# A two-layer spline network: one-sided masks, seven rounded weight tiles of sixteen, and weight differences formed on GpSimd

## Chip, cores and metric

One core of one Trainium2 chip. The time is that of the whole program on the device in microseconds; the figure compared is the median of several runs.

## The reference, cut

```python
h = concat([tokens(x), text(x_txt)])               # 32 x 164 rows of 192
h = h + attention(layernorm(h))
h = h + spline(spline(layernorm(h), w1), w2)       # 192 -> 512 -> 192
# spline(x, w): basis = cubic B-spline of x, 16 control points
#   einsum('ndk,odk->no', basis, w);  w1: (512, 192, 16), w2: (192, 512, 16)
```

The basis has finite width: of the 16 control points four are not zero for a given x. The kernel handles them as four residues r of the control point's index, each with a number n that says which of four places i the value belongs to. So the sum over 16 points is a sum over r and i of mask(n = i) times value(r) times weight(i, r).

## The kernel before

The program runs a stem with a deformed convolution, then attention, then `spline_phase`. Only the last is touched.

**First layer.** 16 pairs of batch items (`PAIRS`), each 328 rows (`PT`). A pair's work on TensorE is eight halves (`HALVES`, j), each with 36 rounded products of 328 columns (L1889 to L1891). VectorE forms the masks of a half (L1666) into a ring of four buffers `f`; `f_used` counts halves that TensorE has read. Each pair VectorE also normalises the pair after next (`norm_in`, `norm_out`), with one `power` and one `double` on GpSimd in between: its program is a loop of these two and nothing else. SP's queue loads rows (`reload`) and stores the hidden values (`leave`, four stores of 164 KB, each behind a wait for ScalarE's `empty`).

**Second layer.** 41 tiles q of 128 rows (`OT`). A tile on TensorE is four steps i; a step is 16 blocks r of 128 inputs (`4 * CH`). The first four blocks (`r < CH`, `SPLIT` = 512 columns) are split: value and weight each as a rounded high half and a low rest. The high value times high and low weight is one rounded product of 384 columns (L1911), the low value times high weight one of 192 (L1913). The other 12 blocks are plain f32 products of 192 columns (L1917), each of which the records show as two. The masked values are the stationary operand, the weights are the moving one.

VectorE's program, `tile2`, makes for each i three masks (`take2`, L1677: high, low, rest) and between them the next tile's values, 2048 columns each: `outer` (L799), `inner` (L803), `value` (L808); at the end `low2` (L1654) and the two additions of `leave` (L1736, L1739) of the tile before. Masks go into rings of four, one buffer for each i; `take2` waits until TensorE has read step i of the tile before. ScalarE works ahead: `after2` (round, `square_inner`) of tile q+2 once the masks of tile q are formed, then `before2` (four positions, three folds, `square_outer`) of tile q+3, then `high2`, which rounds the new value to its high half. Each engine takes its instructions in the order of the program text.

**The passage between the layers.** `w2` (four slices i of 1536 KB) lies where the first layer's high weights were, so slice i is loaded when TensorE has read halves 2i + 2 of the last pair. ScalarE rounds the first four blocks of each slice (`weight2_high`, L1809) and VectorE subtracts (`weight2_low`, L1703). On ScalarE the order is `high2(0,0)`, `before2(0,1,1)`, `weight2_high` 0 and 1, `after2(1,1)`, `weight2_high` 2, `before2(1,2,0)`, `empty`, `weight2_high` 3, `high2(1,1)`. On VectorE tile 0 forms the masks of i = 0, 1, 2, with `outer`, `inner` and `value` of tile 1 between, then weight 0, the mask of i = 3, and weights 1 to 3. The masks' buffers have the first layer's shape of ring, so tile 0's masks can be written from half 5 of the last pair on.

## Time and profile before

| | |
|---|---|
| median of 3 runs | 2402.74 us (2398.84 to 2403.97) |
| profiled execution, time | 2403.18 us |
| profiled execution, span | 2401.5 us |
| mean granted TensorE clock | 0.979 |
| TensorE busy | 2297.5 us, 96% |
| VectorE busy | 1878.7 us, 78% |
| ScalarE busy | 1396.5 us, 58% |
| GpSimd busy | 246.3 us, 10% |

The span runs from the first to the last recorded instruction; the time has 1.7 us more. The second layer is the stretch from 1568.9 us to the end. A matmul's end is modelled in the records and overlaps its successor, so what a product costs is read from start to start.

### The profile page before, as it was taken

The numbers are of one execution on the slowest core, as the hardware profiler recorded it, in microseconds if no ns is written. First come the engines' busy times: TensorE is split into PE (matmuls) and PEld (weight loads), VectorE is DVE, ScalarE is ACT, GpSimd is POOL, SyncE is SP. The second block draws the span as 40 slices with busy tenths as digits, with TensorE's granted clock in tenths as the row PEclk, the third lists the DMA queues.
The fourth block names the chain that finished last, engine by engine and source line by source line (L and its number), as shares of the span: only waits on it lengthen the run. The fifth ranks groups of instructions, "written<-read, shape, count | busy, mean of one in ns | idle before, by whom it ended". The sixth has DMA issues, their size and how long they took to land.

```text
span 2401.5 us, 48862 instructions
## 1 busy us (share of the span) xinstructions
PE 2297.5 (96%) x20033; PEld 2149.7 (90%) x20033; DVE 1878.7 (78%) x2364; ACT 1396.5 (58%) x1391; POOL 246.3 (10%) x133
## 2 busy tenths in 40 slices
PE   6699989999999989999999999989999999999999
PEld 5366777888888789999999999989999999999999
DVE  7699756666666587766767667589999999999995
ACT  5488303444444555435345354678888888888881
POOL 7522100000000021211212111000000000000000
PEclk9799998999999899999999999999999999999999
DMA  6655241111111100000000000210000000000000
GB/s 211 169 153 149 68 154 28 51 47 47 47 47 48 36 20 27 20 21 21 20 27 19 16 27 24 91 59 26 24 22 23 22 22 22 23 23 23 23 19 10
DMA packets 99326, 115.82 MB, mean 48 GB/s; under 512 B 15271, under 2 KB 90551, under 8 KB 98487
## 3 DMA queue, kind: packets, MB, share of 16 engines
q1 hardware_dynamic: 79087, 89.38, 12.4%
q10 hardware_dynamic: 16520, 14.34, 2.0%
q0 software_dynamic: 3616, 10.54, 1.7%
q8 instruction: 87, 1.43, 0.3%
q14 instruction: 16, 0.13, 0.0%
HBM read 83.36 MB, written 30.86 MB: 48 GB/s over the span
## 4 chain that ended last, share of the span: by engine, by line
PE 64%; issue 0%; DVE 0%
PE spline_acc L1917 27%; PE spline_acc L1890 10%; PE spline_acc L1889 10%; PE spline_acc L1891 10%; PE spline_acc L1911 5%; PE spline_acc L1913 2%; PE spline_xT L764 0%; DVE spline_f L1666 0%; DVE spline_weights_low L1649 0%; DVE spline_x L1736 0%; DVE spline_x L1739 0%
## 5 line engine op out<-in xcount | busy, mean ns | idle before, releaser
L1917 PE MATMUL spline_acc<-spline_weights,spline_f 128*128 128x192 f32 x3936 | 672.2, 328 | 0.0
L1917 PEld LDWEIGHTS spline_acc<-spline_weights,spline_f 128*128 128x128 f32 x3936 | 637.4, 190 | 0.0
L1889 PE MATMUL spline_acc<-spline_f,spline_weights_high 128*128 128x328 f32 x1536 | 480.5, 313 | 2.5 <-DVE spline_weights_low L1649 2.5
L1890 PE MATMUL spline_acc<-spline_f,spline_weights_high 128*128 128x328 f32 x1536 | 481.3, 313 | 0.0
L1891 PE MATMUL spline_acc<-spline_f,spline_weights_low 128*128 128x328 f32 x1536 | 477.7, 311 | 0.0
L1889 PEld LDWEIGHTS spline_acc<-spline_f,spline_weights_high 128*128 128x128 f32 x1536 | 289.2, 188 | 2.8 <-DVE spline_weights_low L1649 2.8
L1890 PEld LDWEIGHTS spline_acc<-spline_f,spline_weights_high 128*128 128x128 f32 x1536 | 289.4, 188 | 0.0
L1891 PEld LDWEIGHTS spline_acc<-spline_f,spline_weights_low 128*128 128x128 f32 x1536 | 289.3, 188 | 0.0
L1911 PE MATMUL spline_acc<-spline_weights_split,spline_f_high 128*128 128x384 f32 x656 | 218.2, 389 | 8.2 <-issue 8.2
L1666 DVE SCALAR_TENSOR_TENSOR spline_f<-spline_front 128x984 fp32r<-128x984 f32 x128 | 145.6, 1178 | 100.2 <-PE spline_acc L1891 94.9
L1021 DVE TENSOR_REDUCE attend_max<-scores_by_query 82x6 f32<-82x876 f32 x128 | 135.5, 1059 | 45.2 <-PE scores_by_query L1352 43.0
L1819 ACT ACTIVATE spline_hid<-spline_acc 128x328 f32<-128x328 f32 x64 | 28.1, 445 | 243.7 <-PE spline_acc L1891 243.7
L1913 PE MATMUL spline_acc<-spline_weights_split,spline_f_low 128*128 128x192 f32 x656 | 164.6, 251 | 0.0
L1194 ACT ACTIVATE attend_probs<-scores_by_key 82x1752 f32<-82x1752 f32 x64 | 104.3, 1630 | 90.1 <-PE scores_by_key L1374 90.0
L1666 DVE SCALAR_TENSOR_TENSOR spline_f<-spline_n,spline_a 128x984 fp32r<-128x984 f32 x64 | 75.6, 1181 | 99.9 <-PE spline_acc L1891 99.0
L1677 DVE SCALAR_TENSOR_TENSOR spline_f<-spline_front 128x1536 f32<-128x1536 f32 x84 | 147.1, 1752 | 0.0
L1677 DVE SCALAR_TENSOR_TENSOR spline_f<-spline_n,spline_b 128x1536 f32<-128x1536 f32 x80 | 140.1, 1751 | 0.0
L1911 PEld LDWEIGHTS spline_acc<-spline_weights_split,spline_f_high 128*128 128x128 f32 x656 | 124.0, 189 | 8.5 <-issue 8.5
L1913 PEld LDWEIGHTS spline_acc<-spline_weights_split,spline_f_low 128*128 128x128 f32 x656 | 125.7, 192 | 0.0
L574 ACT ACTIVATE spline_front<-spline_front,pixel_neg 120x576 f32<-120x576 f32 x160 | 109.7, 763 | 22.4 <-DMA spline_front<-pos_scr 22.4
L1784 ACT ACTIVATE spline_s<-spline_xn,spline_offset 128x512 f32<-128x512 f32 x160 | 101.9, 708 | 7.9 <-DMA spline_xn<-hid_scr 6.4
L551 DVE TENSOR_TENSOR hat_weights<-spline_front,spline_weights_raw 120x2880 f32<-120x2880 f32 x32 | 101.1, 3159 | 2.9 <-PE sample_acc L604 0.6
(229 smaller groups left out, 4247.6 us busy)
## 6 DMA issues: line engine op xcount, KB each, us to landing
spline_front<-pos_scr SPq DMA_DIRECT2D x32, 540.0 KB, 4.4
hid_scr<-spline_hid SPq DMA_DIRECT2D x64, 164.0 KB, 1.8
spline_xn<-hid_scr SPq DMA_DIRECT2D x41, 256.0 KB, 3.1
attend_spread<-rec_scr SPq DMA_DIRECT2D x128, 61.5 KB, 2.2
pix_scr<-spline_front SPq DMA_DIRECT2D x32, 225.0 KB
spline_weights_raw<-w SPq DMA_DIRECT2D x1, 6144.0 KB, 21.3
spline_weights<-w SPq DMA_DIRECT2D x4, 1536.0 KB, 6.2
spline_x<-h_scr SPq DMA_DIRECT2D x41, 96.0 KB, 1.9
```

The costliest lines, as they stand in the source:

```text
L574: nc.scalar.activation(dy[u][0:PIXC, part, :].rearrange("p (k n) -> p k n", k=TAPS), p[:, 0], ACT.Abs, bias=neg[0:PIXC, part:part + 1])
L1021: nc.vector.tensor_reduce(mx[0:ROWS, n, 2 * h:2 * h + 2, 0:HG], sc[0:ROWS, :, 0:SW].rearrange("p j (g n) -> p j g n", n=SPAN), AX_X, ALU.m ...
L1194: nc.scalar.activation(prT[0:ROWS, c, :, FROM[c]:FROM[c] + SPAN].rearrange("p (j g) n -> p j g n", j=4), tp[0:ROWS, :, 0:SW].rearrange("p ...
L1666: nc.vector.scalar_tensor_tensor(f[j % RING][:, part * HC:(part + 1) * HC], n_[u][:, cols], MAGIC + i, v[:, cols], ALU.is_equal, ALU.mult) ...
L1677: nc.vector.scalar_tensor_tensor(dst[:], n, MAGIC + i, v, ALU.is_equal, ALU.mult).then_inc(f_ready, 1)
L1784: nc.scalar.activation(dst[:, r * HID:(r + 1) * HID].rearrange("p (c n) -> p c n", c=CH), x2[u], ACT.Identity, bias=bias2[:, r:r + 1], sca ...
L1889: nc.tensor.matmul(z, high, x_high, start=start, stop=False)
L1890: nc.tensor.matmul(z, high, x_low, start=False, stop=False)
L1891: last = nc.tensor.matmul(z, low, x_high, start=False, stop=stop)
L1911: nc.tensor.matmul(acc2[:, u, 0:2 * D], f_high[i][:, cols], w2_split[:, i, r].rearrange("p s o -> p (s o)"), start=start, stop=False)
L1913: last = nc.tensor.matmul(z, f_low[i][:, cols], w2_split[:, i, r, 0, :], start=False, stop=False)
L1917: last = nc.tensor.matmul(z, f_rest[i][:, cols], w2[:, i, r, :], start=False, stop=stop)
```

## The change

- Masks of the second layer are one-sided: n >= i instead of n = i. The weights of slice i become the difference w2[i] - w2[i-1], so that the sum is the same. The masks for i = 0 are always one, so TensorE takes `v_high`, `v_low` and `b` themselves as operands. Values have the other sign (`minus_value`), and `leave` multiplies by -1/6.
- Seven blocks of 16 (`SETS`) are split instead of four; nine stay f32. `SPLIT` is 896 columns, the rest 1152.
- The differences for i = 1 to 3 are formed in the first layer: 36 times, SP loads two pieces of 128 x 256 from `w2`, GpSimd subtracts, SP stores the result in `step_scr`.
- The second layer's memory is laid out anew. Mask buffers exist for i = 1 to 3 only and are written once the whole first layer has been read. The raw weights of the seven blocks and the nine plain ones are loaded by separate DMAs; `weight2_high` i waits for halves 6, 7, 8, 8 of the last pair; the low halves are written over the raw ones, and lie 21.5 KB behind the high ones of the same block.
- `after2` waits, from tile 2 on, until TensorE has done step 0 of the tile two before, since it overwrites `b`.
- The orders of ScalarE and VectorE in tile 0 change.

```diff
+    SETS = 7
+    SPLIT = SETS * P
+    L1F, L1U, L2F = 2 * HALVES, HALVES, 9
+    PART = 256
+    HIGH_AT = HALVES * HALF * HID - 4 * SETS * D
...
+        HIGH_FREE = [HALVES * (PAIRS - 1) - (-(HIGH_AT + (i + 1) * SETS * D) // (HALF * HID)) for i in range(4)]
+        RAW_FREE = [HALVES * (PAIRS - 1) - (-(i + 1) * SETS * D // (HALF * HID)) for i in range(4)]
...
+            def load_step(k):
+
+                sp.dma_start(step_to[:], w2_flat[:, bass.ds(k * PART + 16 * D, PART)]).then_inc(step_in, 16)
+                sp.dma_start(step_from[:], w2_flat[:, bass.ds(k * PART, PART)]).then_inc(step_in, 16)
+
+            def leave_step(k):
+
+                sp.wait_ge(step_ready, k + 1)
+                sp.dma_start(step_flat[:, bass.ds(k * PART, PART)], step_to[:]).then_inc(step_out, 16)
+                sp.wait_ge(step_out, 16 * k + 16)
+
             reload(2)
-            with sp.Fori(0, PAIRS - 3) as t:
+            load_step(0)
+            reload(3)
+            leave(0)
+            with sp.Fori(1, PAIRS - 4) as t:
                 reload(t + 3)
-                leave(t)
+                for n in range(3):
+                    leave_step(3 * t - 3 + n)
+                    load_step(3 * t - 2 + n)
+                    if n == 1:
+                        leave(t)
...
             for i in range(4):
-                sp.wait_ge(f_used, HALVES * (PAIRS - 1) + 2 * i + 2)
-                sp.dma_start(w2[:, i], a["w2"][:, i]).then_inc(w2_in[i], 16)
+                sp.wait_ge(f_used, RAW_FREE[i])
+                sp.dma_start(w2_raw[:, i], w2_from[i][:, 0:SETS].rearrange("p r o -> p (r o)")).then_inc(w2_raw_in[i], 16)
+            for i in range(4):
+                sp.wait_ge(f_used, REST_FREE[i])
+                sp.dma_start(w2[:, i], w2_from[i][:, SETS:4 * CH]).then_inc(w2_in[i], 16)
...
-            with pool.Fori(2, PAIRS) as t:
+            def step(k):
+
+                pool.wait_ge(step_in, 32 * k + 32)
+                pool.tensor_tensor(step_to[:], step_to[:], step_from[:], ALU.subtract).then_inc(step_ready, 1)
...
+            with pool.Fori(4, PAIRS) as t:
+                for n in range(3):
+                    step(3 * (t - 4) + n)
                 front.power(pool, t)
                 front.double(pool, t)
...
-                if i == 0:
-                    dve.wait_ge(low_ready, PAIRS + q + 1)
-                dve.wait_ge(f_used, L1U * PAIRS + 4 * q + i - RING + 1)
+                dve.wait_ge(f_used, L1U * PAIRS + (4 * q + i - 3 if not (isinstance(q, int) and q == 0) else 0))
...
-                    nc.vector.scalar_tensor_tensor(dst[:], n, MAGIC + i, v, ALU.is_equal, ALU.mult).then_inc(f_ready, 1)
+                    if i == 1 and dst is f_low[1]:
+                        dve.wait_ge(low_ready, PAIRS + q + 1)
+                    nc.vector.scalar_tensor_tensor(dst[:], n, MAGIC + i, v, ALU.is_ge, ALU.mult).then_inc(f_ready, 1)
+
+            def minus_value(q, u):
+
+                dve.wait_ge(front.outer_ready, PAIRS + q + 1)
+                dve.wait_ge(front.inner_ready, PAIRS + q + 1)
+                nc.vector.scalar_tensor_tensor(b_[u][:], a_[u][:], 0.0, b_[u][:], ALU.min,
+                                               ALU.subtract).then_inc(v_ready, 1)
...
-                take2(q, u, 0)
+                if first:
+                    weight2_low(0)
+                    weight2_low(1)
+                take2(q, u, 1)
                 if more:
                     front.outer(nc, dve, PAIRS + q + 1, a_[v][:], t_[v][:])
-                take2(q, u, 1)
+                if first:
+                    weight2_low(2)
+                take2(q, u, 2)
                 if more:
                     front.inner(nc, dve, PAIRS + q + 1, b_[v][:], t_[v][:])
-                take2(q, u, 2)
-                if more:
-                    front.value(nc, dve, PAIRS + q + 1, a_[v][:], b_[v][:])
+                    minus_value(q + 1, v)
                 if first:
-                    dve.wait_ge(f_used, W2_LOW_FREE)
-                    weight2_low(0)
+                    weight2_low(3)
                 take2(q, u, 3)
-                if first:
-                    for i in range(1, 4):
-                        weight2_low(i)
...
+                if not (isinstance(q, int) and q < 2):
+                    act.wait_ge(f_used, L1U * PAIRS + 4 * q - 7)
                 front.square_inner(nc, act, PAIRS + q, b_[u][:], t_[u][:])
...
             high2(0, 0)
+            weight2_high(0)
+            weight2_high(1)
             act.wait_ge(f_ready, L1F * PAIRS)
             before2(0, 1, 1)
-            weight2_high(0)
-            weight2_high(1)
             after2(1, 1)
             weight2_high(2)
...
-                    pe.wait_ge(f_ready, L1F * PAIRS + 12 * q + 3 * i + 3)
-                    if i == 0 and not first:
-                        pe.wait_ge(y_ready, q - 1)
+                    if i == 0:
+                        pe.wait_ge(low_ready, PAIRS + q + 1)
+                        if not first:
+                            pe.wait_ge(y_ready, q - 1)
+                        high, low, rest = v_high[u], v_low[u], b_[u][:, SPLIT:C2_]
+                    else:
+                        pe.wait_ge(f_ready, L1F * PAIRS + L2F * q + 3 * i)
+                        high, low, rest = f_high[i], f_low[i], f_rest[i]
                     for r in range(4 * CH):
...
+                            both = w2_split[:, :, i, r * D:(r + 1) * D]
+                            nc.tensor.matmul(acc2[:, u, 0:2 * D], high[:, cols], both, start=start, stop=False)
+                            last = nc.tensor.matmul(z, low[:, cols], both[:, 0], start=False, stop=False)
```

## Rows read from the trace of the kernel before

**Rows 1.** The page's busy time (us, share of the span, instructions) by engine.
```profile
PE 2297.5 (96%) x20033; PEld 2149.7 (90%) x20033; DVE 1878.7 (78%) x2364; ACT 1396.5 (58%) x1391; POOL 246.3 (10%) x133
```

**Rows 2.** TensorE's waits, 800 to 2401: line, what for, us, times, longest.
```profile
PE spline_acc L1911 <- issue: 8.2, 1, 8.2
```

**Rows 3.** TensorE's timeline, second layer: start us, length us, line, operation.
```profile
1799.85 4.09 PE L1917 MATMUL spline_acc<-spline_weights,spline_f 128*128 128x192 f32 x24
1803.64 0.47 PE L1911 MATMUL spline_acc<-spline_weights_split,spline_f_high 128*128 128x384 f32 x1
...
1804.04 0.36 PE L1911 MATMUL spline_acc<-spline_weights_split,spline_f_high 128*128 128x384 f32 x1
...
1804.89 4.09 PE L1917 MATMUL spline_acc<-spline_weights,spline_f 128*128 128x192 f32 x24
```

**Rows 4.** TensorE's timeline, where the first layer ends and the second begins.
```profile
1560.31 0.31 PE L1891 MATMUL spline_acc<-spline_f,spline_weights_low 128*128 128x328 f32 x1
1568.85 0.66 PE L1911 MATMUL spline_acc<-spline_weights_split,spline_f_high 128*128 128x384 f32 x1 [8.23 <-issue]
...
1576.84 0.47 PE L1911 MATMUL spline_acc<-spline_weights_split,spline_f_high 128*128 128x384 f32 x1
```

**Rows 5.** Windows of that passage: us, busy us by engine, PEclk, DMA.
```profile
1568.80:1571.00 2.20, 2.15 (x8) 2.18 (x9) 2.20 (x3) 2.17 (x4) 0.00 (x0) 0.50 0.03 7
```

**Rows 6.** VectorE's timeline, second layer, parts of one tile.
```profile
1805.22 1.75 DVE L1677 SCALAR_TENSOR_TENSOR spline_f<-spline_front 128x1536 f32<-128x1536 f32 x1
1806.89 2.29 DVE L803 SCALAR_TENSOR_TENSOR spline_b<-spline_t,spline_b 128x2048 f32<-128x2048 f32 x1
1809.09 0.68 DVE L1677 SCALAR_TENSOR_TENSOR spline_f_high<-spline_front,spline_v_high 128x512 fp32r<-128x512 f32 x1
...
1817.04 0.69 DVE L1654 TENSOR_TENSOR spline_v_low<-spline_b,spline_v_high 128x512 fp32r<-128x512 f32 x1
1817.64 0.35 DVE L1736 SCALAR_TENSOR_TENSOR spline_x<-spline_acc,spline_x 128x192 f32<-128x192 f32 x1
...
1819.10 0.69 DVE L1677 SCALAR_TENSOR_TENSOR spline_f_high<-spline_n,spline_v_high 128x512 fp32r<-128x512 f32 x1 [0.71 <-PE spline_acc L1917]
```

**Rows 7.** ScalarE's timeline, last tile of layer one and tile 0.
```profile
1542.82 2.56 ACT L1784 ACTIVATE spline_s<-spline_xn,spline_offset 128x512 f32<-128x512 f32 x4 [1.49 <-DVE spline_f L1666]
...
1553.36 1.57 ACT L1809 ACTIVATE spline_weights_split<-spline_weights 128x768 fp32r<-128x768 f32 x2
1554.83 1.90 ACT L775 ACTIVATE spline_n<-spline_s 128x2048 f32<-128x2048 f32 x1
...
1560.38 0.82 ACT L1809 ACTIVATE spline_weights_split<-spline_weights 128x768 fp32r<-128x768 f32 x1
1567.62 2.56 ACT L1784 ACTIVATE spline_s<-spline_xn,spline_offset 128x512 f32<-128x512 f32 x4 [6.41 <-DMA spline_xn<-hid_scr]
...
1578.13 1.42 ACT L1819 ACTIVATE spline_hid<-spline_acc 128x328 f32<-128x328 f32 x4
```

**Rows 8.** VectorE's timeline, layer one: two masks, each after a half.
```profile
1522.95 1.19 DVE L1666 SCALAR_TENSOR_TENSOR spline_f<-spline_n,spline_a 128x984 fp32r<-128x984 f32 x1 [3.11 <-PE spline_acc L1891]
...
1528.34 1.18 DVE L1666 SCALAR_TENSOR_TENSOR spline_f<-spline_n,spline_a 128x984 fp32r<-128x984 f32 x1 [3.11 <-PE spline_acc L1891]
```

**Rows 9.** GpSimd and VectorE side by side, layer one.
```profile
1008.53 2.20 DVE L799 SCALAR_TENSOR_TENSOR spline_front<-spline_front 128x1968 f32<-128x1968 f32 x1
...
1008.78 6.51 POOL L745 COPY spline_xn<-spline_xn 82x256 f32<-82x256 f32 x1 [4.63 <-DVE spline_xn L686]
1046.86 1.00 POOL L739 TENSOR_TENSOR spline_rstd<-spline_ve,spline_half 82x4 f32<-82x4 f32 x1 [31.57 <-DVE spline_ve L674]
```

**Rows 10.** The page's DMA issues: KB each, median us to landing.
```profile
hid_scr<-spline_hid SPq DMA_DIRECT2D x64, 164.0 KB, 1.8
...
spline_weights<-w SPq DMA_DIRECT2D x4, 1536.0 KB, 6.2
spline_x<-h_scr SPq DMA_DIRECT2D x41, 96.0 KB, 1.9
```

94 lines of the change are left out of this document (54 added, 40 removed).

## The prediction

> **What bounds the kernel now.** I read the page first: TensorE is busy 96% of the span, VectorE 78% [rows 1]. The list of TensorE's waits then has one large entry after 860 us, 8.2 us ahead of L1911, the first matmul of the second layer [rows 2]. So both spline layers are bound by TensorE, apart from the passage between them. The timeline of the second layer gives its unit, the step: one of a tile's four values of i, 16 products. Twelve are f32, two records each: 24 records from 1799.85 to 1803.64 us, 3.79 us, 0.316 us a product. Four are rounded pairs (L1911 with L1913): 1803.64 to 1804.89 us, 1.25 us, of which the first pair has 0.40 and the other three 0.85, 0.283 each [rows 3]. A step is 5.04 us, a tile 20.16.
>
> The passage [rows 4]: layer one's last matmul starts at 1560.31 us, layer two's first at 1568.85, and the next step at 1576.84. The first step takes 7.99 us, 2.95 more than 5.04: the granted clock there is 0.50, the 1.2 GHz level, after 8.2 us without work [rows 5]. From 1576.84 on there are 163 steps of 5.04 us, which end at 2398.4; the span is 2401.5. So nothing waits in them, and tile 1 starts at 1576.84 + 3 x 5.04 = 1591.96.
>
> VectorE is nearly full in layer two [rows 6], start to start: low2 (512 columns) 0.60 us, a mask over 512 columns the same by the length of its record (0.68 against 0.69), over 1536 columns 1.67, an operation over 2048 columns 2.20, leave 0.75. Four steps of 2.87, three operations of 2.20 and the rest make 19.4 of 20.16; the 0.71 idle is the wait for TensorE. ScalarE has before2 10.54 us, after2 5.55 [rows 7] and high2.
>
> **The change, part by part.**
>
> *More rounded pairs (TensorE).* Three of twelve f32 products become pairs: 0.316 - 0.283 = 0.033 us each, 0.098 a step, so a step is 4.94 us and a tile 19.77. This is on the path for every step that doesn't wait; over the 160 steps of tiles 1 to 40 it is -15.6 us. The high half's moving operand changes its form: 384 columns in one piece before, now two runs of 192, 21.5 KB apart. No row shows that form. I price it at nothing, since the columns are as many; the first pair's excess of 0.12 us over the others [rows 3] is the nearest sign of what a change of stream can cost, so the bounds are 0 and 0.12 a pair. A gain is excluded, as it reads the same columns. I take 0.
>
> *Masks (VectorE).* From 512 and 1536 columns a column costs (1.67 - 0.60)/1024 = 1.04 ns. 896 columns then take 1.00 us, 1152 take 1.27, and one step's masks 3.28. i = 0 needs none any more (TensorE reads v_high, v_low and b), so three steps make 9.84 instead of 11.5. outer, inner and minus_value are 6.6, low2 1.0, leave 0.75; minus_value now stands right behind inner, on whose end it waits: 2.29 - 2.20, 0.1 more. The sum is 18.3 us against TensorE's 19.8: slack 1.5 where it was 0.7. No cost on the path. Uncovered, an excess over 19.8 would count whole, 40 times.
>
> *Waits.* take2(q, 1) waits until TensorE is two steps into tile q-1 and heads VectorE's queue there. Counted from the start of tile q-1 on TensorE: take2(q,1) 9.9 to 13.2, outer, take2(q,2), inner, minus_value until 23.2, take2(q,3) to 26.5, low2(q+1) to 27.5. TensorE wants them at 24.7, 29.7, 34.6 and 39.5, so 8 to 12 us spare. In after2, square_inner waits for TensorE to have read b of tile q-2, which is 4.9 us into that tile; after2 begins later, at 6.7, behind that tile's last masks. Behind it in ScalarE's queue stand before2 and high2; ScalarE's sum is 10.54 + 5.55 + about 0.95 = 17.0 of 19.8. Nothing.
>
> *GpSimd and SP in layer one.* Per pair 3 differences over 256 columns, 6 loads and 3 stores of 128 KB. GpSimd's queue has power and double behind them; SP's has reload ahead and leave(t) after the third load, with leave_step(3t-1) behind. A load or a store of such a size takes 1.9 or 1.8 us [rows 10]; a half takes 5.39 us [rows 8], a pair 43.1. The difference isn't in the trace. Nearest: double's copy of 256 columns, 6.51 us [rows 9], as long as it is because VectorE's operations run beside it; double that for two inputs, 13.0, is the upper end, and about 1 us (that copy without its delay) the lower. At 6.5 us a chain of store, load and difference is 10.2 us, three are 31 of 43: hidden, and power is wanted only some 38 us after double begins, 1008.78 to 1046.86 [rows 9]. VectorE beside the copy takes 2.20 us for 1968 columns [rows 9], no more than elsewhere, and waits 3.11 us in most halves [rows 8]. Price nothing, a gain excluded as TensorE bounds. The Trainium skill (GPSIMD Engine Reference, Key points) says that GpSimd shares its SBUF interfaces with VectorE and contends with its instructions of two SBUF inputs. By that rule the masks would be held up by the 36 differences; the trace shows the copy stretched and the mask beside it not, so by the row the charge is nothing, and by the rule it would still fall into VectorE's 3.11 us.
>
> *The passage.* Weights: the raw weights of the seven tiles are asked for after halves 1 to 4 of the last pair, the other nine's after halves 5 to 8; 884 KB land within the 6.2 us of 1536 KB [rows 10], so they are there. Halves end at 1549.8, 1555.2 and 1560.6 (steps of 5.39 back from the last). A ScalarE copy of 1344 columns is interpolated between 0.82 us at 768 and 1.90 at 2048 [rows 7]: 1.3 us, bounds 0.8 and 1.9; the subtraction on VectorE 1.5.
> - ScalarE: weight2_high(0) at 1549.8, (1) at 1555.2 to 1556.5. Only then before2(0,1,1), which ran at 1542.82 before: 1556.5 + 10.54 = 1567.1; after2(1,1) to 1572.6; weight2_high(2) to 1573.9; before2(1,2,0) to 1584.4; empty 1.4 to 1585.8; weight2_high(3) to 1587.1. The wait on the half thus moves this whole queue 13.7 us back.
> - VectorE: take2(0,0,1) must wait for layer one's end, 1560.6 to 1563.9. weight2_low(2), for ScalarE until 1573.95, to 1575.5; take2(0,0,2) to 1578.9. inner and minus_value to 1583.4; weight2_low(3) 1587.1 to 1588.6; take2(0,0,3) to 1592.0.
> - TensorE: i = 0 needs only the values and weights 0, ready by 1552.6, so it starts at 1560.5 with no wait: the 8.2 us and its 2.95 are gone. i = 0 and 1 end at 1570.4. Late next is i = 2: 1578.9, 8.5 us idle, and again a step at the low clock, 7.9 us, to 1586.8. Then i = 3 at 1592.0, 5.2 us idle. If the clock falls here too the step ends at 1599.9, else at 1597.0. I take the first, as the one wait of this length in the second layer's rows had it.
> - Tile 1 then starts at 1599.9, not 1591.96: +7.9 us. Its masks are ready at 1596.2, 1601.7 and 1609.5, against a need of 1604.8, 1609.8 and 1614.7, so no further wait.
>
> **Sum.** Profiled span 2401.5 - 15.6 + 7.9 = 2393.8, plus the 1.7 us around it = 2395.5, against 2403.18 profiled. That lies 0.44 over the median of the three runs, so 2395 for a median.
>
> **The rivals.**
> 1. *The clock doesn't fall in the second gap of tile 0.* For: it is 5.2 us against 8.2. Against: the step ahead of it has only just been at work. Tile 1 starts at 1597.0: 2392.
> 2. *The passage costs more or less than by interpolation*: the copies at their bounds move ScalarE's queue by 0.5 us each, and a longer idle before i = 2 makes nothing up. Up to +4 us: 2399. For: every term is a chain over three engines. Against: all its long terms have rows.
> 3. *A pair with a moving operand in two runs costs more.* This is the rival on the other side. One pair in each step's seven, 1120 in tiles 1 to 40, so 10 ns a pair are 11 us. The gain is gone at 7 ns and the kernel is slower by 0.2% from 11 ns on; at 20 ns the time is 2417. For: the first pair's 0.12 us. Against: that goes with the change from f32, and happens once a step now as before.
> 4. *GpSimd is late in layer one*, by the rule of contention above: from 43.1/3 - 3.7 = 10.7 us a difference, three chains are longer than a pair. At 13.0 it would be 50 of 43, 12 times, +84 us: 2479. For: the copy's 6.51 us. Against: VectorE idles in nearly every half and lets it through. The Trainium skill (GPSIMD Engine Reference, Elementwise — side-by-side cycle accounting) has 4.5 us for a sum of 2048 columns, an estimate of 0.6 for 256.
>
> **How the numbers follow.** Forecast 0.50, rival 1 0.16, rival 2 0.17, rival 3 0.13, rival 4 0.04. The predicted time is the likeliest case's, 2395. A measurement of this kernel can tell about 0.2%, 4.8 us, so faster means below 2397.9, slower above 2407.5. Rival 1 is faster, the forecast in nine of ten (it is 2.4 us from the line), rival 2 mostly same, rival 3 partly same and mostly slower. That gives faster 0.63, same 0.23, slower 0.14. The range: below, rival 1 with copies at their lower bound and the runs' spread of 2.5, 2389; above, rival 2 and the nearest part of rival 3, 2403.
>
> **What would show it.** Right: starts of steps 4.94 us apart, pairs 0.28 (rival 3: more); VectorE waiting some 1.5 us a tile, at the first mask of a tile; TensorE going on at once after layer one, then waiting about 8 us before i = 2 and 5 before i = 3 of tile 0, for VectorE's masks, with VectorE waiting there for ScalarE's weight copies; the clock at 0.50 behind both (rival 1: behind the first alone); pairs of layer one 43.1 us apart as before (rival 4: more). Wrong: a wait of TensorE in a later tile, or VectorE over 19.8 us a tile.

## The result

| | kernel before | changed kernel |
|---|---|---|
| median of 20 runs | 2397.55 us (2387.64 to 2403.97) | 2385.51 us (2376.12 to 2396.35) |
| profiled execution, time | 2403.18 us | 2391.56 us |
| profiled execution, span | 2401.5 us | 2389.8 us |

The ratio of changed to before is 0.9952, with a 95% interval of 0.9938 to 0.9966: the change makes the kernel 0.5% faster. I had forecast 2395 us, in a range of 2389 to 2403, against a median of 2402.74: a ratio of 0.9968. The direction is right, the time lies 3.5 us under the range.

**The profile after.** The page's line of busy time (as [rows 1]) and TensorE's waits from 800 us on (as [rows 2]; columns: who waited for whom, us in total, times, longest):

```profile
PE 2277.9 (95%) x20033; PEld 2134.9 (89%) x20033; DVE 1846.9 (77%) x2241; ACT 1411.4 (59%) x1391; POOL 302.1 (13%) x169
```

```profile
PE spline_acc L1977 <- DVE spline_f L1726: 14.8, 2, 8.5
```

One wait of 8.2 us has become two that make 14.8, for masks of VectorE. TensorE's timeline of the passage (as [rows 4]), L1977 being the high product of a pair and L1981 the f32 product:

```profile
1558.41 0.31 PE L1951 MATMUL spline_acc<-spline_f,spline_weights_low 128*128 128x328 f32 x1
1558.56 0.33 PE L1977 MATMUL spline_acc<-spline_weights_split,spline_v_high 128*128 128x384 f32 x1
...
1577.03 0.66 PE L1977 MATMUL spline_acc<-spline_weights_split,spline_f_high 128*128 128x384 f32 x1 [8.48 <-DVE spline_f L1726]
...
1590.07 0.66 PE L1977 MATMUL spline_acc<-spline_weights_split,spline_f_high 128*128 128x384 f32 x1 [6.28 <-DVE spline_f L1726]
...
1596.82 0.47 PE L1977 MATMUL spline_acc<-spline_weights_split,spline_v_high 128*128 128x384 f32 x1
```

Layer two follows on layer one at once. The step i = 2 of tile 0 begins after 8.48 us without work, i = 3 after 6.28. The record at 1596.82 is the first product of tile 1. Windows of that passage (us, busy us of each engine, granted clock, DMA share, GB/s; as [rows 5]):

```profile
1558.00:1573.00 15.00, 10.55 (x69) 10.26 (x67) 6.60 (x5) 14.87 (x10) 0.00 (x0) 1.00 0.25 78
1573.60:1580.00 6.40, 2.97 (x11) 3.00 (x12) 6.30 (x6) 6.30 (x5) 0.00 (x0) 0.50 0.00 0
1580.00:1587.00 7.00, 3.79 (x22) 3.50 (x21) 3.39 (x3) 5.87 (x8) 0.00 (x0) 0.97 0.37 121
1587.00:1594.00 7.00, 3.93 (x15) 3.96 (x16) 7.00 (x7) 4.01 (x3) 0.00 (x0) 0.52 0.17 50
```

The clock is at 1.00 for the first two steps, at 0.50 (the 1.2 GHz level) behind the first wait, up again soon after 1580 us, and low again behind the second. What the waits hang on is in the timelines of ScalarE (as [rows 7]) and VectorE:

```profile
1553.43 1.33 ACT L1869 ACTIVATE spline_weights_split<-spline_weights_raw 128x1344 fp32r<-128x1344 f32 x1 [4.06 <-PE spline_acc L1951]
1554.66 2.54 ACT L1842 ACTIVATE spline_s<-spline_xn,spline_offset 128x512 f32<-128x512 f32 x4
...
1570.72 1.31 ACT L1869 ACTIVATE spline_weights_split<-spline_weights_raw 128x1344 fp32r<-128x1344 f32 x1
1571.93 2.55 ACT L1842 ACTIVATE spline_s<-spline_xn,spline_offset 128x512 f32<-128x512 f32 x4
...
1582.43 1.42 ACT L1879 ACTIVATE spline_hid<-spline_acc 128x328 f32<-128x328 f32 x4
1583.72 1.34 ACT L1869 ACTIVATE spline_weights_split<-spline_weights_raw 128x1344 fp32r<-128x1344 f32 x1
```

```profile
1558.76 1.09 DVE L1726 SCALAR_TENSOR_TENSOR spline_f_high<-spline_front,spline_v_high 128x896 fp32r<-128x896 f32 x1 [2.41 <-PE spline_acc L1951]
...
1572.06 1.56 DVE L1762 TENSOR_TENSOR spline_weights_split<-spline_weights_raw,spline_weights_split 128x1344 fp32r<-128x1344 f32 x1 [4.46 <-ACT spline_weights_split L1869]
1573.53 1.08 DVE L1726 SCALAR_TENSOR_TENSOR spline_f_high<-spline_front,spline_v_high 128x896 fp32r<-128x896 f32 x1
...
1585.09 1.56 DVE L1762 TENSOR_TENSOR spline_weights_split<-spline_weights_raw,spline_weights_split 128x1344 fp32r<-128x1344 f32 x1 [3.61 <-ACT spline_weights_split L1869]
1586.57 1.08 DVE L1726 SCALAR_TENSOR_TENSOR spline_f_high<-spline_front,spline_v_high 128x896 fp32r<-128x896 f32 x1
```

ScalarE does weight 1 at 1553.43, then ten microseconds of positions and folds and another five of after2, and only at 1570.72 weight 2; weight 3 comes at 1583.72. VectorE waits 4.46 and 3.61 us for them (L1762), and its masks (L1726) stand behind. The steady part, TensorE (as [rows 3]) and VectorE's first mask of two tiles (as the last line of [rows 6]):

```profile
1801.34 3.11 PE L1981 MATMUL spline_acc<-spline_weights,spline_f 128*128 128x192 f32 x18
1804.15 0.47 PE L1977 MATMUL spline_acc<-spline_weights_split,spline_f_high 128*128 128x384 f32 x1
...
1806.26 3.11 PE L1981 MATMUL spline_acc<-spline_weights,spline_f 128*128 128x192 f32 x18
1809.07 0.47 PE L1977 MATMUL spline_acc<-spline_weights_split,spline_f_high 128*128 128x384 f32 x1
...
1811.21 3.11 PE L1981 MATMUL spline_acc<-spline_weights,spline_f 128*128 128x192 f32 x18
```

```profile
2102.62 2.95 PE spline_acc L1981 x18
...
2379.07 2.95 PE spline_acc L1981 x18
```

```profile
1804.49 1.09 DVE L1726 SCALAR_TENSOR_TENSOR spline_f_high<-spline_front,spline_v_high 128x896 fp32r<-128x896 f32 x1 [1.38 <-PE spline_acc L1981]
...
1824.23 1.09 DVE L1726 SCALAR_TENSOR_TENSOR spline_f_high<-spline_n,spline_v_high 128x896 fp32r<-128x896 f32 x1 [1.38 <-PE spline_acc L1981]
```

The second fence is from the chain that ended last (start, us, engine, line). Between its two lines lie 56 steps in 276.45 us: 4.937 us a step, where it was 5.04. In the first of these fences the seven pairs of one step take 2.11 us and those of the next 2.14. VectorE now waits 1.38 us for TensorE in each tile, 19.74 us apart.

**Where the time went.** Measured between fixed points of the two profiled executions. The first and last start of one of layer one's three products stand ahead of the semicolon, before and after:

```profile
L1889 PE MATMUL spline_acc<-spline_f,spline_weights_high x1536: 309/311/643, 859.7 to 1560.0; 128*128 128x328 f32 x192
```

```profile
L1949 PE MATMUL spline_acc<-spline_f,spline_weights_high x1536: 308/310/643, 857.5 to 1558.1; 128*128 128x328 f32 x192
```

| stretch | before | after | difference |
|---|---|---|---|
| start to layer one's first product | 859.7 | 857.5 | -2.2 |
| layer one, first to last start | 700.3 | 700.6 | +0.3 |
| passage, end of layer one to tile 1 (1560.5 to 1592.0; 1558.6 to 1596.8) | 31.5 | 38.2 | +6.7 |
| tiles 1 to 40 | 806.3 | 789.9 | -16.4 |

The last two are the change: -9.7 us. The first row is smaller than the spread that the experiments show for it, so it can't be put down to the change.

### The profile page after: what moved, and what is told of

It reads as the page before. It is cut to its first block, busy times and chain, and to the rows that moved or that the text cites. A ratio compares the mean times of both kernels' runs of the same rounds, so it can differ in the third digit from the quotient of the medians.

```text
span 2389.8 us, 49107 instructions
## 1 busy us (share of the span) xinstructions
PE 2277.9 (95%) x20033; PEld 2134.9 (89%) x20033; DVE 1846.9 (77%) x2241; ACT 1411.4 (59%) x1391; POOL 302.1 (13%) x169
## 4 chain that ended last, share of the span: by engine, by line
PE 62%; ACT 1%; DVE 0%; issue 0%; ACTq 0%
PE spline_acc L1981 20%; PE spline_acc L1950 10%; PE spline_acc L1949 10%; PE spline_acc L1951 9%; PE spline_acc L1977 9%; PE spline_acc L1978 4%; PE spline_xT L764 0%; ACT spline_s L1842 0%; ACT spline_weights_split L1869 0%; DVE spline_f L1715 0%; ACT spline_t L778 0%; ACT spline_t L780 0%; ACT spline_front L778 0%; ACT spline_front L780 0%; ACT spline_t L782 0%
## 5 line engine op out<-in xcount | busy, mean ns | idle before, releaser
L1949 PE MATMUL spline_acc<-spline_f,spline_weights_high 128*128 128x328 f32 x1536 | 480.6, 313 | 2.5 <-DVE spline_weights_low L1698 2.5
L1981 PE MATMUL spline_acc<-spline_weights,spline_f 128*128 128x192 f32 x2214 | 382.7, 327 | 0.0
L1981 PEld LDWEIGHTS spline_acc<-spline_weights,spline_f 128*128 128x128 f32 x2214 | 356.8, 190 | 0.0
L1949 PEld LDWEIGHTS spline_acc<-spline_f,spline_weights_high 128*128 128x128 f32 x1536 | 290.7, 189 | 2.8 <-DVE spline_weights_low L1698 2.8
L1977 PE MATMUL spline_acc<-spline_weights_split,spline_f_high 128*128 128x384 f32 x861 | 274.0, 382 | 14.8 <-DVE spline_f L1726 14.8
L1978 PE MATMUL spline_acc<-spline_weights_split,spline_f_low 128*128 128x192 f32 x861 | 217.8, 253 | 0.0
L1977 PEld LDWEIGHTS spline_acc<-spline_weights_split,spline_f_high 128*128 128x128 f32 x861 | 163.8, 190 | 15.3 <-issue 15.3
L1978 PEld LDWEIGHTS spline_acc<-spline_weights_split,spline_f_low 128*128 128x128 f32 x861 | 166.5, 193 | 0.0
L745 POOL COPY spline_xn<-spline_xn 82x256 f32<-82x256 f32 x16 | 94.2, 5886 | 72.7 <-DVE spline_xn L686 72.7
L604 PE MATMUL sample_acc<-hat_weights,spline_x 120*96 120x288 f32 (+1 forms) x320 | 84.1, 419 | 19.5 <-DVE hat_weights L551 18.4
```

What stands on the lines that cost most here:

```text
L1949: nc.tensor.matmul(z, high, x_high, start=start, stop=False)
L1977: nc.tensor.matmul(acc2[:, u, 0:2 * D], high[:, cols], both, start=start, stop=False)
L1978: last = nc.tensor.matmul(z, low[:, cols], both[:, 0], start=False, stop=False)
L1981: last = nc.tensor.matmul(z, rest[:, cols], w2[:, i, r - SETS, :], start=False, stop=stop)
```

## Experiments

The measure that hardly moves from one execution to the next is the stretch from layer one's last L1889 (or its like) to layer two's last f32 product: 838.3 us before (1560.0 to 2398.3), 828.6 after (1558.1 to 2386.7). It is called layer two's length below. A kernel that was timed several times beside the kernel before has a ratio to it too.

**The changed kernel again.**

> The changed kernel itself, as the reference point for the runs beside it. Its profiled execution had a step of 4.937 us in the second layer, waits of TensorE of 8.5 and 6.3 us in tile 0, and 1596.8 - 1558.6 = 38.2 us from the end of layer one to the start of tile 1 (before: 31.5). Theory: the steps give -16.5 us, the passage costs +6.7, what lies ahead of layer one belongs to the execution and not to the change, so the ratio to the kernel before is (2402 - 10)/2402 = 0.996. Rival: something ahead of layer two got faster with the change (1.9 us earlier in the one profiled execution); then the ratio is 0.995 and the first matmul of layer two starts earlier in this execution too, by about 2 us against the run of the kernel before.

Measured: ratio 0.9968 (0.9949 to 0.9987), 828.6 us of layer two again, waits that make 14.8 us as before. Layer one's first product started at 857.3. The rival asked for a start 2 us ahead of the kernel before's; one start is no proof of that, and the next paragraph shows why. The two ratios, 0.9952 and 0.9968, overlap, and the -9.7 us of the traces (0.9960) lies between them.

**What lies ahead of layer one.** Of each trace, the line of L604, the first large stretch of products near 100 us (lengths in ns, least, median and greatest, then first and last start). Kernel before, changed kernel, better order and no differences (both below):

```profile
L604 PEld LDWEIGHTS sample_acc<-hat_weights,spline_x x320: 159/163/285, 102.4 to 264.3; 120*96 120x96 f32 x128, 96*96 96x96 f32 x32
```

```profile
L604 PEld LDWEIGHTS sample_acc<-hat_weights,spline_x x320: 159/163/284, 100.2 to 262.6; 120*96 120x96 f32 x128, 96*96 96x96 f32 x32
```

```profile
L604 PEld LDWEIGHTS sample_acc<-hat_weights,spline_x x320: 159/163/283, 92.2 to 254.3; 120*96 120x96 f32 x128, 96*96 96x96 f32 x32
```

```profile
L604 PEld LDWEIGHTS sample_acc<-hat_weights,spline_x x320: 159/163/283, 108.9 to 270.7; 120*96 120x96 f32 x128, 96*96 96x96 f32 x32
```

The code ahead of layer one is the same in all of them, and L604 starts at 102.4, 100.2, 92.2 and 108.9 us, layer one at 859.7, 857.5, 846.9 and 868.0. In the twelve profiled executions of this study L604 starts between 92.2 and 109.1 us, a spread of 17, and layer one between 846.9 and 868.0. So 21 us of spread are there before any changed line. Not all of it arises early: from L604 to layer one takes 752.1 to 763.7 us, and the two executions with L604 at 96.0 and 107.5 both start layer one near 859.7.

Ten of the twelve have their chip on record, and the starts go with it: 846.9 to 857.3 us in four on one chip, 859.6 and 859.7 in two on a second, 865.1 to 868.0 in four on a third. The kernel before had a median of 2396.59, 2403.55 and 2405.31 us on these three. What makes the difference wasn't tried. In the first 110 us the execution of the better order had the granted clock at 0.88 and the last one 0.81, and DMA's share was 0.72 and 0.65.

**The better order.** Edit (ScalarE; and VectorE's tile 0):

```diff
             high2(0, 0)
-            weight2_high(0)
-            weight2_high(1)
             act.wait_ge(f_ready, L1F * PAIRS)
             before2(0, 1, 1)
+            for i in range(4):
+                weight2_high(i)
             after2(1, 1)
-            weight2_high(2)
             before2(1, 2, 0)
+            high2(1, 1)
             empty(PAIRS - 1)
-            weight2_high(3)
-            high2(1, 1)
...
                 take2(q, u, 2)
+                if first:
+                    weight2_low(3)
+                    take2(q, u, 3)
                 if more:
                     front.inner(nc, dve, PAIRS + q + 1, b_[v][:], t_[v][:])
                     minus_value(q + 1, v)
-                if first:
-                    weight2_low(3)
-                take2(q, u, 3)
+                if not first:
+                    take2(q, u, 3)
```

> The changed kernel with another order in the passage: ScalarE does before2(0,1,1) first and then all four weight2_high, high2(1,1) ahead of empty; VectorE does weight2_low(3) and the masks of i = 3 ahead of inner and minus_value of tile 1. Theory (the two waits of tile 0 come from ScalarE's queue behind the weight copies): worked out from the profile after, the four copies end at 1561.3 instead of 1585.1, masks 2 are ready at 1569.0 (wanted 1568.5), masks 3 at 1573.9, and tile 1's values at 1580.5 (wanted 1579). So waits of TensorE of 0.5 and 2 us instead of 8.5 and 6.3, no fall of the clock, tile 1 starts at about 1580.6 instead of 1596.8: 16 us less than the changed kernel, 26 less than before (ratio to before about 0.989). Rival (the weights themselves are late, by DMA): the waits stay above 5 us, for the weights instead of the masks, and the time falls by under 5 us.

Measured: ratio 0.9894 (0.9865 to 0.9923), layer two 814.0 us, 14.6 less than the changed kernel. TensorE's timeline:

```profile
1557.96 0.41 PE L1977 MATMUL spline_acc<-spline_weights_split,spline_f_high 128*128 128x384 f32 x1 [0.66 <-DVE spline_f L1726]
...
1569.32 0.44 PE L1977 MATMUL spline_acc<-spline_weights_split,spline_v_high 128*128 128x384 f32 x1 [1.25 <-DVE spline_v_low L1703]
...
1585.94 0.45 PE L1977 MATMUL spline_acc<-spline_weights_split,spline_f_high 128*128 128x384 f32 x1 [1.60 <-DVE spline_f L1726]
```

Three waits of 0.66, 1.25 and 1.60 us are left; after each the lengths of products are those of the full clock. It follows that the two long waits were queueing of ScalarE and VectorE, not the weights' DMAs. The third small wait, in tile 1, I had not worked out.

**ScalarE's half of that order alone.**

Edit: the first part of the diff above, with empty left ahead of high2(1,1); VectorE as in the changed kernel.

> The changed kernel with ScalarE's order alone changed (before2(0,1,1), then the four weight copies, then after2); VectorE's order is that of the changed kernel. Theory: masks of i = 2 are ready 10.4 us after layer one's end, against a need after 9.9; those of i = 3 wait behind inner, minus_value and weight2_low(3), 19.6 us after the end against a need after 15.4: waits of 0.6 and 4.3 us, and TensorE's clock may fall once. Tile 1 starts some 25 us after layer one's end against 38.2 in the changed kernel: 12 to 13 us less than it, ratio to before 0.990 to 0.992. Rival (it was VectorE's order that held both waits): less than half of that.

Measured: ratio 0.9924 (0.9897 to 0.9950), layer two 817.5 us, 11.1 less than the changed kernel; waits 0.66 and 4.15 us. The waits are as worked out; the saving is a little under the expected 12 to 13. The clock fell behind the 4.15 us, which I had only called possible, and the step there took 7.21 us, 2.3 more than 4.94. ScalarE's order held most of the time, VectorE's the rest (3.5 us).

**Three moves more.** Edit, on top of the better order:

```diff
-            before2(1, 2, 0)
-            high2(1, 1)
+            act.wait_ge(n_ready, PAIRS + 2)
+            position(1, 2, 0, s_)
+            act.wait_ge(v_ready, PAIRS + 1)
+            front.folds(nc, act, PAIRS + 2, s_, t_[0][:])
+            high2(1, 1)
+            front.square_outer(nc, act, PAIRS + 2, a_[0][:], t_[0][:])
             empty(PAIRS - 1)
...
+                if first:
+                    front.outer(nc, dve, PAIRS + q + 1, a_[v][:], t_[v][:])
                 take2(q, u, 1)
-                if more:
+                if more and not first:
                     front.outer(nc, dve, PAIRS + q + 1, a_[v][:], t_[v][:])
...
-                if first:
-                    weight2_low(3)
-                    take2(q, u, 3)
+                ahead = isinstance(q, int) and q < 2
+                if first:
+                    weight2_low(3)
+                if ahead:
+                    take2(q, u, 3)
```

> The changed kernel with the better order of the passage (the four weight copies together on ScalarE, weight 3 and the masks of i = 3 early on VectorE) and three moves more: outer of tile 1 ahead of the first masks, where VectorE had waited 2.4 us for layer one's end; high2(1,1) ahead of square_outer on ScalarE; in tile 1, too, the masks of i = 3 ahead of inner and minus_value. In the profile of the kernel with the better order three waits of TensorE were left, 0.66, 1.25 and 1.60 us. Theory (all three are VectorE's and ScalarE's queues, and each move shifts them by its own length): no wait over 0.5 us is left, layer two takes 3 to 3.5 us less than with the better order, 810.5 to 811 us from layer one's last matmul to layer two's last (changed kernel 828.6, better order 814.0); ratio to before 0.988. Rival (minus_value or high2 then are late for tile 2, since they are formed last): a wait of 1 to 2 us moves to the first matmul of tile 2 and at most 1.5 us are won.

Measured: ratio 0.9877 (0.9850 to 0.9904), layer two 812.8 us. Its waits:

```profile
1599.93 0.45 PE L1985 MATMUL spline_acc<-spline_weights_split,spline_v_high 128*128 128x384 f32 x1 [0.69 <-DVE spline_x L1803]
...
1616.55 0.45 PE L1985 MATMUL spline_acc<-spline_weights_split,spline_f_high 128*128 128x384 f32 x1 [1.55 <-DVE spline_f L1726]
```

The waits in tiles 0 and 1 are gone, and two have come in tile 2, 0.69 us for the additions of leave and 1.55 for its masks of i = 3. So the rival holds in the main: 1.2 us are won, not 3 to 3.5. I read it so (it isn't tried by itself) that VectorE starts the layer late and catches up by its slack alone, and a reordered queue passes the lateness on. Its ratio is the best of the study, but its interval and the better order's overlap.

**Four split blocks instead of seven.** Edit: SETS = 4.

> The changed kernel with four split blocks instead of seven (one-sided masks, differences on GpSimd, and the new passage stay). Theory (the gain of the steady part is that of the three converted products alone): the step goes back to 5.04 us (0.10 more), so 160 steps cost 16.5 us more; the passage stays within 1 us of the changed kernel's. Time: 16 us over the changed kernel, about +6 over the kernel before, ratio to before 1.002 to 1.003. Rival (the split moving operand makes each pair dearer, partly hiding a larger gain of each conversion): the step is 5.05 to 5.08, as four pairs then cost more than before's 1.25 us.

Measured: ratio 1.0020 (1.0000 to 1.0041), layer two 844.4 us, 15.8 more than with seven. TensorE:

```profile
1801.93 0.47 PE L1977 MATMUL spline_acc<-spline_weights_split,spline_f_high 128*128 128x384 f32 x1
...
1803.18 4.09 PE L1981 MATMUL spline_acc<-spline_weights,spline_f 128*128 128x192 f32 x24
1806.97 0.47 PE L1977 MATMUL spline_acc<-spline_weights_split,spline_f_high 128*128 128x384 f32 x1
```

A step is 5.04 us again and four pairs take 1.25, as before. So the whole gain of the steady part is that of three conversions a step; the one-sided masks and differences by themselves change nothing on the path there. The passage is still the new one, and the kernel is no faster than the one before.

**The moving operand in two runs, in the kernel before.** Edit:

```diff
-                        [("spline2_weights_split", [P, 4, CH, 2, D], F32R)])
+                        [("spline2_weights_split", [P, 2, 4, CH * D], F32R)])
...
-                                             w2_split[:, i, r].rearrange("p s o -> p (s o)"), start=start, stop=False)
+                                             w2_split[:, :, i, r * D:(r + 1) * D], start=start, stop=False)
```

> The kernel before, with the split weights laid out so that the 384 columns of a high product are two runs of 192, 12 KB apart, instead of one. Nothing else changes. Theory: the form of the moving operand costs nothing; the step stays 5.04 us and the time is the kernel before's within 0.1%. Rival: a pair costs 4 to 9 ns more (in the changed kernel the pairs behind the first are 0.288 to 0.292 us apart, in the kernel before 0.283); then four pairs add 0.02 to 0.036 us a step, 3 to 6 us in all (0.1 to 0.25%), and starts of pairs are 0.288 apart here too.

Measured: ratio 1.0005 (0.9983 to 1.0027), layer two 837.7 us against 838.3. TensorE:

```profile
1802.38 0.36 PE L1912 MATMUL spline_acc<-spline_weights_split,spline_f_high 128*128 128x384 f32 x1
...
1803.23 4.09 PE L1918 MATMUL spline_acc<-spline_weights,spline_f 128*128 128x192 f32 x24
1807.02 0.47 PE L1912 MATMUL spline_acc<-spline_weights_split,spline_f_high 128*128 128x384 f32 x1
```

Three pairs take 0.85 us (1802.38 to 1803.23), a step 5.04 (1801.98 to 1807.02). Two runs 12 KB apart cost nothing, and the 0.12 us that I had let them cost falls. The four-block kernel above has this form too, and its pairs are as cheap. For the changed kernel's seven blocks it isn't settled: at 0.40 us for the first pair and 0.283 for each of the others seven pairs would take 2.10 us, but over the steps from 1700 to 2340 us they take 2.107 for i = 0 and 2, 2.140 for i = 1 and 3, the same in each tile. That is 3.8 us over tiles 1 to 40, on the path. So the pairs are dearer, as rival 3 had it, but by 1 to 7 ns only. Whether that is the 21.5 KB between the runs, the place of the slices or something else wasn't tried.

**More masks on VectorE.** Edit, ahead of the masks of i = 3:

```diff
+                if i == 3:
+                    for k in range(7):
+                        if not (isinstance(q, int) and q == 0 and k == 0):
+                            dve.wait_ge(spare_done, 7 * q + k)
+                        nc.vector.scalar_tensor_tensor(spare_mask[:], n_[u][:, 0:256], MAGIC,
+                                                       v_high[u][:, 0:256].bitcast(F32), ALU.is_ge, ALU.mult
+                                                       ).then_inc(spare_done, 1)
```

> The changed kernel with seven more small masks on VectorE in every tile (256 columns each, into an unused buffer, each behind a wait for the one before it), 3.1 us in all: about what the three masks of i = 0 would cost with seven split blocks. It asks whether the one-sided masks carry anything. Theory: VectorE has 18.3 us of work a tile against 19.75 of TensorE; with 3.1 more it is the bound at 21.4, so every tile takes about 1.7 us more, some 65 us over 39 tiles, and TensorE waits for masks in every tile; time about 2455. Without the one-sided masks seven split blocks would thus be slower than before. Rival (VectorE's slack is larger than its record shows): the time stays within 20 us of the changed kernel's.

Measured (one timed run): 2465.05 us, layer two 894.7 us, 66 more than the changed kernel. Waits of TensorE from 1640 to 2370 us:

```profile
PE spline_acc L1985 <- DVE spline_f L1734: 48.5, 34, 1.6
```

Tiles are 21.5 us apart (waits at 2006.74 and 2028.25). The added masks stand for those of i = 0. By this run seven split blocks gain only because the masks of i = 0 are gone: that is what the one-sided masks carry, though they save nothing themselves.

**No differences.** Edit (the second layer then multiplies by the weights themselves):

```diff
-            load_step(0)
...
-                for n in range(3):
-                    leave_step(3 * t - 3 + n)
-                    load_step(3 * t - 2 + n)
-                    if n == 1:
-                        leave(t)
+                leave(t)
...
-            w2_from = [a["w2"][:, 0]] + [step_scr[:, i] for i in range(3)]
+            w2_from = [a["w2"][:, i] for i in range(4)]
...
-                for n in range(3):
-                    step(3 * (t - 4) + n)
```

> The changed kernel without the 36 differences of weights: GpSimd subtracts nothing, SP loads and stores nothing for it, and the second layer multiplies by the weights themselves (so its sums are other ones; the work of all engines in layer two is the same). Theory: the differences cost nothing on the path; layer one takes 700 us from its first to its last matmul here as in the changed kernel and in the kernel before (700.6 and 700.3), and the time is the changed kernel's within 0.1%. VectorE's masks of layer one come back from 1199 to 1178 ns on average, since GpSimd's 0.74 us then no longer hold up an operation beside it, and its waits for TensorE grow by as much. Rival (SP's or GpSimd's queue delays norm or turn): layer one is shorter by 1 us or more.

Measured: ratio 0.9956 (0.9931 to 0.9981), beside 0.9952 and 0.9968 of the changed kernel; layer two 829.5 us. Layer one takes 699.2 us, 1.4 less, which looks like the rival. It is the clock: over the first 20 us from layer one's first product the windows are, changed kernel and this one,

```profile
857.50:877.50 20.00, 20.00 (x115) 20.00 (x116) 19.82 (x24) 19.87 (x18) 2.79 (x1) 0.85 0.06 19
```

```profile
868.00:888.00 20.00, 20.00 (x124) 20.00 (x125) 19.82 (x24) 19.87 (x18) 2.79 (x1) 0.92 0.03 9
```

0.85 is 6.0 us at half clock, 0.92 is 3.2, a difference of 2.8 us in low clock, 1.4 of time. The kernel before with the two-run operand, which has no differences either, has 0.92 and 699.2 too; the kernel before has 0.86 and 700.3. And the kernel with three moves more, which has the differences, has 0.91 over its first 20 us and takes 699.4. So the differences cost nothing on the path. What they do to VectorE is in the changed kernel's trace, two of its operations beside GpSimd's subtraction (L1683):

```profile
1013.24 2.92 DVE L808 TENSOR_TENSOR spline_front<-spline_front 128x1968 f32<-128x1968 f32 x1
...
1018.28 2.19 DVE L812 TENSOR_TENSOR spline_front<-spline_front 128x1968 fp32r<-128x1968 f32 x1
```

```profile
1013.36 0.74 POOL L1683 TENSOR_TENSOR spline_step_to<-spline_step_to,spline_step_from 128x256 f32<-128x256 f32 x1
1018.84 2.22 POOL L1683 TENSOR_TENSOR spline_step_to<-spline_step_to,spline_step_from 128x256 f32<-128x256 f32 x1 [4.75 <-DMA spline_step_from<-w]
```

L808 takes 2.92 us, where it is 2.21 before: longer by 0.7, about GpSimd's own 0.74. L812 isn't lengthened; there it is the subtraction that takes 2.22 us. The masks of layer one take some 1200 ns on average with the differences and 1179 without. All this falls into the 3.11 us that VectorE waits in most halves.

**The old passage in a better order.** Edit, in the kernel before (VectorE's tile 0, `inner` and `value` shortened; ScalarE):

```diff
                 take2(q, u, 1)
+                if first:
+                    dve.wait_ge(f_used, W2_LOW_FREE)
+                    weight2_low(0)
+                    weight2_low(1)
...
                 take2(q, u, 2)
+                if first:
+                    weight2_low(2)
...
-                if first:
-                    dve.wait_ge(f_used, W2_LOW_FREE)
-                    weight2_low(0)
                 take2(q, u, 3)
                 if first:
-                    for i in range(1, 4):
-                        weight2_low(i)
+                    weight2_low(3)
...
             weight2_high(2)
+            weight2_high(3)
             before2(1, 2, 0)
             empty(PAIRS - 1)
-            weight2_high(3)
```

> The kernel before with only the order of the passage changed: VectorE subtracts weights 0 and 1 ahead of inner, weight 2 behind the masks of i = 2, ScalarE rounds weight 3 right behind weight 2. It asks how much of a better passage has nothing to do with the change. Worked out from the profile of before: weights 0 ready 1.1 us after layer one's end instead of 8.3, no fall of the clock, later one wait of about 2 us for the masks of tile 1. Theory: 8 us less than before (ratio 0.9967); so of the 26 us between before and the changed kernel in its better order some 8 are of the order alone and some 16 to 17 of the seven split blocks. Rival (the low clock after the gap would come anyway, or the weights are late by DMA): under 4 us.

Measured: ratio 0.9992 (0.9971 to 1.0014), layer two 834.3 us, 4.0 less than before. The wait ahead of layer two is 1.10 us instead of 8.23, but another came:

```profile
1589.63 0.69 PE L1913 MATMUL spline_acc<-spline_weights_split,spline_f_high 128*128 128x384 f32 x1 [3.12 <-DVE spline_f L1677]
```

```profile
1589.60:1592.00 2.40, 2.37 (x9) 2.37 (x10) 2.40 (x2) 2.40 (x3) 0.00 (x0) 0.50 0.38 111
```

The wait at tile 1 is 3.12 us, 1 us more than worked out, and behind it the clock is low. So I was wrong on half of it: the order alone is worth 4.0 us in the trace, and the ratio shows no gain clear of noise. Of the 24.3 us between the kernel before and the better order (838.3 to 814.0) some 20 are then beyond what this order gave.

**Products in TensorE's gaps.** Edit, in TensorE's tile 0:

```diff
+                        if i > 1:
+                            for n in range(48 if i == 2 else 44):
+                                nc.tensor.matmul(xT[:, 0, 0:2 * D], w2_split[:, 0, 1, 0:P], w2_split[:, :, 1, 0:D],
+                                                 start=True, stop=True)
                         pe.wait_ge(w2_ready, i + 1)
```

> The changed kernel in its own order, with 48 and 44 products of 384 columns that go to an unused bank put into TensorE's two waits of tile 0 (7.8 and 7.2 us at 0.163 us each), so that it does not idle there. It asks what of the two gaps is the low clock. Theory: the masks come as before, the granted clock stays at 1.00 through both steps, which lose nothing (4.94 us instead of 6.6 each in the changed kernel), and the second wait is longer by what the first step gained, since the masks of i = 3 do not move. Tile 1 then starts only by the second step's 1.7 us earlier: 827 us from layer one's last matmul to layer two's last, against 828.6. Rival (both steps' clock losses are on the path, as priced in the sum of the prediction's alternative): 825.3 us.

Measured (one timed run): 2391.50 us, layer two 826.8 us, 1.8 less than the changed kernel; from layer one's last L1949 on, i = 2 starts after 18.9 us (18.9 there), i = 3 after 32.0 (32.0), tile 1 after 36.9 (38.7). The products take 0.18 us each and end 0.17 and 0.24 us ahead of the masks, so they hold nothing up. Clock:

```profile
1575.00:1580.00 5.00, 4.83 (x29) 4.54 (x29) 5.00 (x5) 4.93 (x5) 0.00 (x0) 1.00 0.00 0
...
1590.00:1595.00 5.00, 4.76 (x31) 4.47 (x30) 5.00 (x6) 3.25 (x2) 0.00 (x0) 1.00 0.16 46
```

The clock stays at 1.00, and only the second step's loss was on the path: 1.8 us. Behind the first wait the low clock is free, since i = 3 waits for VectorE anyway.

## Why the prediction was right and where it wasn't

- *A step from 5.04 to 4.94 us; -15.6 us.* Right: 4.937, -16.4. A conversion is worth 0.103/3 = 0.034 us, where I had 0.033. Both terms are larger than I had them, and nearly cancel: six records fewer (3.79 less 2.81 us) are 0.98, 0.327 for an f32 product where I took its mean of 0.316, and seven pairs take 4.937 - 2.81 = 2.13 us on average, so each added one (2.13 - 1.25)/3 = 0.29 where I took 0.283. That two errors met is luck.
- *VectorE 18.3 of 19.8, slack 1.5.* Right: 1.38 us of wait in each tile. That this is the next limit is shown by the added masks, +66 us.
- *Two runs of the moving operand: nothing.* Right for two runs 12 KB apart, shown by the kernel before with that form. In the changed kernel the pairs behind the first cost 0.285 to 0.290 us instead of 0.283, 3.8 us in all, which the price of nothing had wrong; why is open. My bound of 0.12 us a pair came from the first pair's excess, and that is no cost: the f32 products' 0.316 is a mean that is short by as much, as the 0.327 shows.
- *The passage.* The chain is right to 0.2 us for each term: from layer one's end (1558.7 us) ScalarE's weight 2 starts after 12.0 us (12.0 forecast), the masks of i = 2 end after 18.2 (18.3), those of i = 3 after 31.2 (31.4). The size wasn't: +7.9 forecast, +6.7 measured. The term that was mis-sized is the step behind the second wait: 7.9 us forecast, as [rows 4] had it, and 6.8 measured (1590.07 to 1596.82). The products in the gap won 1.8, so that the clock's part on the path is 1.8 us and not 2.95. The step behind the first wait was shorter still, about 6.5 us, off the path. Both waits were there, and the clock fell behind both, so rival 1 did not come.
- *GpSimd and SP in layer one: nothing.* The price is right. The reason was half wrong: I read from one row that VectorE isn't held beside GpSimd. It can be, by 0.7 us beside a subtraction of two inputs. The rule of the Trainium skill (GPSIMD Engine Reference, Key points), that GpSimd contends with VectorE's instructions of two SBUF inputs, is what this trace shows. In [rows 9] it was GpSimd that waited (the copy takes 6.51 us, and 0.39 where it is shortest), and that row says nothing on what VectorE loses when it is the one to wait. The subtraction itself takes 0.73 to 2.56 us, with a median of 1.69, not 6.5.
- *The sum.* In the traces -9.7 us against -7.7: 0.8 from the steps, 1.2 from the passage.
- *The step that failed: from the sum to the median, and the range.* The time is below the range because the level it was counted from moved. I had put the profiled execution 0.44 us above the median of three runs and the runs' spread at 2.5 us. The three runs lay between 2398.84 and 2403.97; twenty lie between 2387.64 and 2403.97, with a median of 2397.55, 5.2 lower. The traces show a spread of that size ahead of the change: layer one starts anywhere from 846.9 to 868.0 us, mostly by the chip. Which chip the three runs and the twenty were on isn't on record, so whether the level moved by the chip or by chance stays open. Of the 9.5 us between 2395 and 2385.5 this level is 5.2, the sum 2.0, and 2.3 are left: the medians of twenty runs differ by 12.0 us where the traces have 9.7, within the interval (8.2 to 14.9 us). With -7.7 on 2397.55 the forecast would have been 2389.9, and a range with 5 us more below would have held 2385.5. As a ratio, my low end (2389 on 2402.74, 0.9943) held the measured 0.9952.
- *What stays open.* Whether the change moves anything ahead of layer one. The traces give 0.9960, the timed runs 0.9952 and 0.9968, so nothing asks for it; with executions 21 us apart it can't be seen either. Why the stretch ahead of layer one differs that much, between chips and between executions, wasn't tried.

## What to carry to other kernels

Where a chain of two engines feeds a third, look at the change from one stage to the next instruction by instruction: a wait for the last half of a stage, put ahead of independent work in a queue, made TensorE wait 14.8 us here. Another order gave back 14.6 us, more than the 9.7 that the change itself had won. Ask, too, for the spread of the stretch ahead of the change before trusting three runs, and for the chip: compare between fixed points inside the trace.

## What the hardware showed that I had not expected

- The clock fell behind a wait of 3.12 us (granted 0.50 afterwards), and not behind waits of 0.66 to 1.60. What the step behind a wait lost doesn't follow the wait's length: about 1.5 us behind 8.48 and 1.8 behind 6.28 (changed kernel), 2.3 behind 4.15 (ScalarE's half), 2.95 behind 8.23 (kernel before).
- VectorE's L808 of two inputs is lengthened by a subtraction on GpSimd beside it, by 0.7 us, about the other's whole length of 0.74. Beside L812 it is the other way round: VectorE's 2.19 us stay, and the subtraction takes 2.22.
- Laying the 384 moving columns in two runs 12 KB apart costs TensorE nothing: pairs stay 0.283 us apart (kernel before, edited, and the four-block kernel). With seven blocks, where the runs are 21.5 KB apart, pairs are 0.285 apart in i = 0 and 2 and 0.290 in i = 1 and 3, cause not shown.
- The same code reaches layer one after 847 to 857 us on one chip and after 865 to 868 on another, and the kernel before has medians of 2396.59 and 2405.31 us there.
